# A macaron layer with routed experts on one core: weights sent by SyncE behind x, row numbers read and fetched by GpSimd, and a new order of the work

## The chip, the cores and the metric

The kernel runs on one core of a Trainium2 chip. The metric is device time in microseconds of one execution, the median of several. Five engines have work: TensorE (PE; its weight loads are PEld), VectorE (DVE), ScalarE (ACT), GpSimd (POOL) and SyncE (SP), which only issues transfers. Each engine runs its instructions in order, and a wait at the head of an engine holds all that is queued behind it.

## The reference

x has 8 sequences of 512 tokens of 256 numbers, 4,096 tokens in all. The layer is feed-forward, attention, feed-forward, each added to x:

```python
x = x + 0.5 * ffn(layernorm(x), gate_w, w1, w2, w3)
x = x + attn(layernorm(x), W_q, W_k, gain, bias, log_mix, log_scale)
x = x + 0.5 * ffn(layernorm(x), gate_w, w1, w2, w3)   # the same weights again
```

`ffn` scores 8 experts per token, keeps the best two, and for these two computes `w2 @ (silu(w1 @ t) * (w3 @ t))` with an inner width of 512, weighted and summed. `attn` compares each token with the earlier ones of its sequence (x·x), keeps the 8 most alike, takes a softmax over q·k of these, blends the mean of their vectors with x, and passes gain, bias and a gelu. Both need the whole precision of float32 in the choice of experts and of neighbours, so the kernel splits numbers into a high and a low float16 part and multiplies three times.

## The kernel before

**The two feed-forward layers** (L = 0 and 1) are computed only for chosen experts. Tokens are taken in "subtiles" of 512 (8 per layer, n = 0 to 7 for L = 0 and 16 to 23 for L = 1): layer norm (`stats`, `aggr` on DVE, the root `root` on POOL at L903, `shift` on DVE, `normal` and `nhi` on ACT, `low` on DVE), the gate (`flip`, `flop`, `score`), the choice (`rcopy`, `rtop`, `rsel`, `rank`, `rpos`). Then `scatter` writes each token's row (high and low parts and the token's number) to a list of its expert in DRAM, `hs`, by indirect transfers of POOL (L921): two of 128 rows for each `scatter`, 32 `scatter` and so 64 transfers a layer. The second choice (k = 1) first waits until the first choice's transfers of the same rows have landed, since it rewrites the token numbers in place (L918).

**Tables and tiles.** `table` computes on DVE which expert and which 128 rows each tile takes. Layer 0 has two tables: the first after the first quarter of the tokens is known, for tiles 0 to 8; the second needs all 64 transfers and nine padding writes (`pads`, SP), and serves tiles 9 to 70. `line` (SP) copies a table's row numbers into one partition, `rows` (SP, L1008) loads them into registers of SP, up to four tiles at a time. There are 71 tiles a layer, 142 in all, numbered through. For each tile n:

- `load` on SP: wait for the scatters and for the buffer, then turn 128 rows of `hs` into `HT` (ring of 3) by a transposing transfer (L991), and fetch the 128 row numbers into `IDX` (ring of 8) by a plain one of 4 bytes a row (L995);
- `up` on PE (L1161): two halves of 6 products of 512 columns; `tanh` (silu, ACT L1289), `gate` (DVE L1654), `high` (ACT L1298), `glow` (DVE L1660);
- `gt` on SP (L1031): a transposing transfer into `GH` (ring of 3); `down` on PE (L1173): 12 products of 256 columns; `evict` (ACT L1305, ring of 3);
- `put` on POOL (L939): an indirect transfer that writes the result rows to `yt`, where the tokens' order is restored.

**The weights** (12.6 MB, six transfers of 2 MB) come in on POOL's queue, issued behind the third `root` (L907). PE sums their squares (`sum`, L1097), DVE makes scales (`scale`), ACT and DVE split each of 24 pieces (`wh`, `wl`; L1239, L1457). The first `up` needs 16 pieces split, the first `gt` and `down` all 24 (`s_wl` 24).

**The middle**: `fetch` (SP L1046) and `join` (DVE L1669) bring a layer's results back into x; for each of 8 sequences the attention steps follow (`ht`, `qk`, `sim`, `sco`, `top`, `veil`, `mask`, `exp`, `phi`, `plo`, `pt`, `msg`, `blend`, and on POOL `affine`, L948 and L951), interleaved with tiles of layer 0 and the routing of layer 1. At the end the joins of layer 1 and the outputs (`out`, SP L1069).

**The order** of all this is one string, `ORDER`, a letter for each step. A small planner (`make_plan`) replays it, checks that each step's predecessors are there, and hands out the PSUM banks and buffers; each engine then runs its own steps in that order.

Of the kernel before, what the change touches and what calls it, by code (L numbers as in the profile page):

```python
# [9 lines left out]
F32 = mybir.dt.float32  # L10
# [17 lines left out]
RING = 8  # L28
# [65 lines left out]
class Want:  # L94
# [9 lines left out]
LAG = 3  # L104
PS = 1
# [147 lines left out]
def make_plan():  # L253
# [224 lines left out]

    def loads():
        for n, (L, j) in enumerate(seq):  # L480
            k = table_for(L, j)
            use["tab", n] = k
            known = (L, KNOWN[L][k])
            r = router_at(*known)
            after = (("table", (L, k)),) + tuple(("scatter", last_scatter(L, f)) for f in range(r[1] + 1))
            after += (("pads", (L, 8)),) if KNOWN[L][k] == NT else ()
            after += (("rows", (head[n],)),)
            yield tile("load", (n,), after + ((("up", (n - 3, 1)),) if n >= 3 else ()) +
                       ((("put", (n - RING,)),) if n >= RING else ()))

# [13 lines left out]
    def tanhs():  # L504
        for n in range(N):
            yield tile("tanh", (n,), (("up", (n, 0)),) + ((("glow", (n - 2,)),) if n >= 2 else ()),
                       gives=(("x", n, 0),))
# [17 lines left out]
    def evicts():  # L525
        for n in range(N):
            yield tile("evict", (n,), (("down", (n,)),) + ((("put", (n - 3,)),) if n >= 3 else ()),
                       gives=(("y", n),))
# [5 lines left out]
    P.run([prepare(), final(), first_routers(), tables(0), tables(1), sums(), scales(), split(), split2(),  # L534
           scalars(), rows(), loads(), whiches(), ups(), downs(), tanhs(), gates(), highs(), glows(), turned(),
# [4 lines left out]
def macaron_kernel(nc, x_d, wk_d, wqk_d, gw_d, gain_d, bias_d, lg_d, out_d, hs_d, yt_d):  # L540
    P, seq = make_plan()
    use, nth = P.use, P.nth
    with ExitStack() as ctx:
# [108 lines left out]
        HT = [sb(f"ht{i}", [128, 512], F16) for i in range(3)]  # L652
        TH = [sb(f"th{i}", [128, 512], F32) for i in range(2)]
# [14 lines left out]
        d_in = [sem(f"d_in{i}") for i in range(3)]  # L668
        d_y = [sem(f"d_y{i}") for i in range(3)]
# [6 lines left out]
        d_gt = [sem(f"d_gt{i}") for i in range(3)]  # L676
# [137 lines left out]
        def stored(n):  # L814

            return [16 * ((n - i) // 3 + 1) for i in range(3)]
# [45 lines left out]
        def _(eng):  # L862
            e = Eng(eng)
            const, marks, zeros = Tick(s_const), Tick(s_mk1), Tick(s_zero)
# [33 lines left out]
            for kind, key in P.order:  # L898
                if kind == "root":
# [24 lines left out]
                elif kind == "zero":  # L924
# [5 lines left out]
                    zeros.on(eng.tensor_copy(PHS[slot][:, PADC:PADC + 18].bitcast(I32), padid[:]))  # L930
                elif kind == "put":
# [4 lines left out]
                    if j > FULL:  # L936
                        e.wait_ge(d_y[(n - 1) % 3], 16 * ((n - 1) // 3 + 1))
# [23 lines left out]
        def _(eng):  # L961
# [9 lines left out]
            for kind, key in P.order:  # L971
# [8 lines left out]
                elif kind == "load":  # L980
# [8 lines left out]
                    if n >= 3:  # L989
                        e.wait_ge(s_x3, n - 2)  # L990
# [793 lines left out]
```

## Time and profile before

| | us |
|---|---|
| median of 3 runs | 896.85 (896.12 to 900.83) |
| the profiled execution | 894.73 |
| its span | 893.0 |
| PE busy | 716.3 (80%) |
| DVE, ACT, POOL busy | 559.7, 512.6, 379.8 |

The span is the time from the first to the last instruction in the trace; the profiled execution's own time is 1.7 us more. "Busy" of POOL does not count its waits, register loads and the issue gaps. A wait is named after the event that ended it.

### The profile page before, as it was taken

What the parts mean: (1) busy time and instruction counts of PE and PEld (TensorE: products, weight loads), DVE (VectorE), ACT (ScalarE), POOL (GpSimd) and SP (SyncE); (2) the same over time, 40 slices, a digit from 0 to 9 for tenths busy, and PEclk for the clock granted to TensorE, in tenths of its full rate; (3) what the DMA queues carried; (4) which work ended last, traced back from release to release, by engine and by line L of the source; (5) the groups of instructions that cost most, each with busy time, mean ns of one, the idle gap of its engine ahead of it and who ended that gap; (6) DMA issues with size and microseconds to landing.
All of it is one profiled execution on the core that took longest, in us unless ns stands there. A gap on an engine that the chain in (4) does not pass through costs nothing. (4 is left out here: it accounts for less than half of the span.)

```text
span 893.0 us, 17410 instructions
## 1 busy us (share of the span) xinstructions
PE 716.3 (80%) x4672; PEld 432.9 (48%) x4672; DVE 559.7 (63%) x1596; ACT 512.6 (57%) x954; POOL 379.8 (43%) x433
## 2 busy tenths in 40 slices
PE   1652425799989998889998798889998889997971
PEld 1551213446645555554555455555554445654641
DVE  6728881233367786786879787888684514335753
ACT  4727831263357896866889688865874323332320
POOL 4447874213322325465365634564364522221211
PEclk9975588899999999999999999999999989999986
DMA  6953237466796878797987877797878677678995
GB/s 239 429 196 93 93 102 169 108 110 140 132 212 116 127 157 135 144 194 158 178 170 181 166 163 145 138 185 150 153 137 166 150 169 142 128 134 234 218 279 178
DMA packets 328213, 147.76 MB, mean 165 GB/s; under 512 B 309501, under 2 KB 312445, under 8 KB 327357
## 3 DMA queue, kind: packets, MB, share of 16 engines
q1 hardware_dynamic: 314301, 97.61, 57.2%
q0 software_dynamic: 13824, 49.04, 16.8%
q8 instruction: 47, 0.77, 0.4%
q14 instruction: 41, 0.34, 0.1%
HBM read 33.96 MB, written 43.14 MB: 86 GB/s over the span
## 5 line engine op out<-in xcount | busy, mean ns | idle before, releaser
L1161 PE MATMUL B<-t_W,t_ht 128*128 x1704 | 406.1, 388 | 49.5 <-DMA t_ht<-hs 38.6
L939 POOL DMA_INDIRECT yt<-t_W,t_idx x142 | 148.8, 1048 | 388.6 <-ACT t_W L1305 338.4
L1161 PEld LDWEIGHTS B<-t_W,t_ht 128*128 128x128 f16 x1704 | 167.4, 99 | 233.7 <-issue 75.8
L1654 DVE SCALAR_TENSOR_TENSOR t_th<-B,t_K,t_th 128x512 f32<-128x512 f32 x142 | 105.9, 748 | 134.5 <-PE B L1161 93.3
L1173 PE MATMUL B<-t_W,t_gh 128*128 x1140 | 142.8, 276 | 24.7 <-DMA t_gh<-t_gp 18.4
L1289 ACT ACTIVATE t_th<-B,t_K 128x512 f32<-128x512 f32 x142 | 96.8, 683 | 106.7 <-PE B L1161 89.1
L1173 PEld LDWEIGHTS B<-t_W,t_gh 128*128 128x128 f16 x1140 | 109.3, 99 | 61.0 <-issue 37.0
L921 POOL DMA_INDIRECT hs<-t_s,t_POS x112 | 117.1, 1045 | 47.7 <-issue 25.5
L1305 ACT ACTIVATE t_W<-B 128x256 f32<-128x256 f32 x142 | 53.1, 374 | 98.1 <-PE B L1173 87.4
L1660 DVE TENSOR_TENSOR t_gp<-t_th,t_gp 128x512 f16<-128x512 f32 x95 | 66.9, 707 | 32.6 <-ACT t_gp L1298 29.0
L1298 ACT ACTIVATE t_gp<-t_th 128x512 f16<-128x512 f32 x95 | 58.8, 624 | 42.1 <-DVE t_th L1654 28.1
L1173 PE MATMUL B<-t_W 128*128 x564 | 71.0, 276 | 5.5 <-ACT t_W L1305 2.9
L1173 PEld LDWEIGHTS B<-t_W 128*128 128x128 f16 x564 | 54.6, 99 | 22.2 <-issue 9.9
L1258 ACT ACTIVATE t_hp<-t_X,t_ve 128x256 f32<-128x256 f32 x96 | 49.5, 590 | 24.5 <-DVE t_ve L1503 24.0
L1660 DVE TENSOR_TENSOR t_W<-t_th,t_W 128x512 f16<-128x512 f32 x47 | 32.7, 695 | 26.7 <-ACT t_W L1298 21.2
L1289 ACT ACT_TABLE_LOAD x31 | 39.8, 1283 | 6.5 <-DVE t_gp L1660 3.6
L1298 ACT ACTIVATE t_W<-t_th 128x512 f16<-128x512 f32 x47 | 29.3, 624 | 21.5 <-DVE t_th L1654 19.4
L1669 DVE SCALAR_TENSOR_TENSOR t_X<-t_hp,t_CW,t_X 128x256 f32<-128x256 f32 x64 | 31.9, 508 | 14.4 <-DMA t_hp<-yt 13.3
L903 POOL TENSOR_TENSOR t_ve<-t_ve,t_mhalf 128x4 f32<-128x4 f32 x24 | 26.9, 1122 | 31.9 <-DVE t_ve L1497 31.1
L1669 DVE SCALAR_TENSOR_TENSOR t_X<-t_s,t_CW,t_X 128x256 f32<-128x256 f32 x64 | 30.4, 488 | 12.7 <-DMA t_s<-yt 11.6
L1514 DVE TENSOR_TENSOR t_s<-t_hp,t_s 128x256 f16<-128x256 f32 x88 | 36.1, 461 | 0.0
L1225 PE MATMUL B<-t_s,t_ph 128*128 128x256 f16 x240 | 31.3, 273 | 4.5 <-DMA t_ph<-t_p 3.8
(205 smaller groups left out, 855.3 us busy)
## 6 DMA issues: line engine op xcount, KB each, us to landing
t_W<-wk POOLq DMA_DIRECT2D x6, 2048.0 KB, 13.3
t_hp<-yt SPq DMA_DIRECT2D x16, 512.0 KB, 4.4
t_s<-yt SPq DMA_DIRECT2D x15, 512.0 KB
t_X<-x SPq DMA_DIRECT2D x8, 512.0 KB, 7.3
out<-t_X SPq DMA_DIRECT2D x7, 512.0 KB, 5.8
hs<-t_ph SPq DMA_DIRECT2D x18, 136.0 KB
t_ht<-hs SPq DMA_TRANSPOSE x142
t_idx<-hs SPq DMA_DIRECT2D x142, 0.5 KB
```

The lines of the kernel that those rows point to most:

```text
L921: eng.indirect_dma_start(hs_d[L], bass.IndirectOffsetOnAxis(ap=POS[:, k, t + j:t + j + 1], axis=0), SROW[slot][:, 2 * h + j, :], None).the ...
L939: eng.indirect_dma_start(yt_d[L], bass.IndirectOffsetOnAxis(ap=IDX[:, n % RING:n % RING + 1], axis=0), YO[n % 3], None).then_inc(d_y[n % 3 ...
L1161: t = eng.matmul(B[b][:], HT[n % 3][:, (2 * hl + db) * 128:(2 * hl + db) * 128 + 128], W16[:, bass.ds(expert[n] * 4096 + (db * 2048 + wl * ...
L1173: t = eng.matmul(B[b][:, 0:256], GH[n % 3][:, gl, fb * 128:fb * 128 + 128], W16[:, bass.ds(expert[n] * 2048 + (W2OFF + wl * 1024 + fb * 25 ...
L1258: eng.activation(hp[:, j, :], X[:, t0 + j, :], ACT.Identity, bias=ve[:, 2, j:j + 1], scale=ve[:, 1, j:j + 1]).then_inc(s_hp, 1)
L1289: eng.activation(TH[n % 2][:], B[b][:], ACT.Silu, scale=K[:, 0:1]).then_inc(free[b], 1)
L1298: eng.activation(GP[n % 3][:, 0, :], TH[n % 2][:], ACT.Copy).then_inc(s_gh, 1)
L1305: eng.activation(YO[n % 3], B[b][:, 0:256], ACT.Copy).then_inc(free[b], 1)
L1514: eng.tensor_tensor(s16[:, j, 256:512], hp[:, j, :], s16[:, j, 0:256], ALU.subtract).then_inc(s_lo, 1)
L1654: eng.scalar_tensor_tensor(out=th[:], in0=B[b1][:], scalar=K[:, 7:8], in1=th[:], op0=ALU.mult, op1=ALU.mult).then_inc(free[b1], 1)
L1660: eng.tensor_tensor(gp[:, 1, :], th[:], gp[:, 0, :], ALU.subtract).then_inc(s_gl, 1)
L1669: xs.on(eng.scalar_tensor_tensor(out=X[:, tile, :], in0=yg[:, k, :], scalar=CW[:, k, tile:tile + 1], in1=X[:, tile, :], op0=ALU.mult, op1= ...
```

## The change

1. **Weights.** POOL no longer issues them behind `root` 2; SP does, behind x, the small weights, lg and bias, at the start.
2. **Row numbers.** `load` on SP keeps only the transposing transfer. The plain transfer into `IDX` becomes a step `ids` on POOL, with the same waits for the scatters, the pads and the buffer. POOL gets the row numbers in registers of its own by a step `places`, which loads them as SP's `rows` does. `rows` stays. `IDX` becomes a ring of 16 instead of 8. `put` now needs `ids` instead of `load`.
3. **Order.** `ORDER` is a new string. The other ring sizes get names (HTR, YR, THR, LAG) and keep their values.

```diff
-RING = 8
+RING = 16
...
+HTR = 3
+YR = 3
+THR = 2
...
+    def place():
+        for i, g in enumerate(groups):
+            L, j = seq[g[0]]
+            yield tile("places", (g[0],), (("line", (L, table_for(L, j))),))
+
+    def idents():
+        for n, (L, j) in enumerate(seq):
+            yield tile("ids", (n,), ready(n) + (("places", (head[n],)),) +
                        ((("put", (n - RING,)),) if n >= RING else ()))
...
-            yield tile("put", (n,), (("evict", (n,)), ("load", (n,))) + ((("put", (n - 1,)),) if seq[n][1] > FULL else ()))
+            yield tile("put", (n,), (("evict", (n,)), ("ids", (n,))) + ((("put", (n - 1,)),) if seq[n][1] > FULL else ()))
...
@@ gpsimd @@
-                    if n == 2:
-                        e.wait_ge(d_x[5], 16)
-                        for i in range(6):
-                            eng.dma_start(W[:, 4 * i + 2:4 * i + 6, :],
-                                          wk_d[:, 4 * i:4 * i + 4, :]).then_inc(d_w[i], 16)
...
+                elif kind == "places":
+                    n, = key
+                    L, j = seq[n]
+                    e.wait_ge(d_line[L][table_for(L, j)], 16)
+                    _, regs = nc.values_load_multi_w_load_instructions(
+                        LINE[L][0:1, j:j + len(group[n])], engines=[mybir.EngineType.Pool], min_val=0, max_val=SPARE,
+                        skip_runtime_bounds_check_because="the table's rows are cut off at the spare one")
+                    place.update(zip(group[n], regs))
+                elif kind == "ids":
+                    n, = key
+                    L, j = seq[n]
+                    k = table_for(L, j)
+                    for s, v in scattered(*router_at(L, KNOWN[L][k])):
+                        e.wait_ge(s, v)
+                    if KNOWN[L][k] == NT:
+                        e.wait_ge(d_pad, 144 * (L + 1))
+                    if n >= RING:
+                        e.wait_ge(d_y[(n - RING) % YR], 16 * ((n - RING) // YR + 1))
+                    eng.dma_start(IDX[:, n % RING:n % RING + 1].bitcast(F16), hs_d[L][bass.ds(place[n], 128), 512:514]
+                                  ).then_inc(d_id[n % RING], 16)
...
@@ sync @@
             eng.dma_start(bias[:], bias_d).then_inc(d_bias, 16)
+            for i in range(6):
+                eng.dma_start(W[:, 4 * i + 2:4 * i + 6, :], wk_d[:, 4 * i:4 * i + 4, :]).then_inc(d_w[i], 16)
...
-                    if n >= 3:
-                        e.wait_ge(s_x3, n - 2)
-                    eng.dma_start(HT[n % 3][:].rearrange("p (a b) -> p a b", a=4), hs_d[L][bass.ds(row, 128), 0:512],
-                                  transpose=True).then_inc(d_in[n % 3], 16)
-                    if n >= RING:
-                        e.wait_ge(d_y[(n - RING) % 3], 16 * ((n - RING) // 3 + 1))
-                    eng.dma_start(IDX[:, n % RING:n % RING + 1].bitcast(F16), hs_d[L][bass.ds(row, 128), 512:514]
-                                  ).then_inc(d_id[n % RING], 16)
+                    if n >= HTR:
+                        e.wait_ge(s_x3, n - HTR + 1)
+                    eng.dma_start(HT[n % HTR][:].rearrange("p (a b) -> p a b", a=4), hs_d[L][bass.ds(row, 128), 0:512],
+                                  transpose=True).then_inc(d_in[n % HTR], 16)
```

The two strings, read engine by engine, hold the same steps but for 38 `places` and 142 `ids`. Where they differ most, around the end of layer 0's scatters (steps numbered in order on their engine; `scatter` 31 is the last of layer 0):

```
POOL before: ... scatter25 scatter26 scatter27 put0 scatter28 scatter29 put1 put2 scatter30 put3 put4 scatter31 put5 put6 ...
POOL after:  root5 places0 scatter6 ... scatter13 root7 ids0 places1 ids1 scatter14 places2 ids2 scatter15 ...
             ... scatter27 scatter28 put0 scatter29 places3 put1 scatter30 ids3 ids4 ids5 scatter31 put2 put3 ids6 ids7
             places4 ids8 ids9 ids10 ids11 put4 places5 ids12 ids13 ids14 places6 put5 ...
SP before:   load2 rows2 load3 gt0 load4 load5 pads0 pads1 line1 gt1 ... gt5 pads8 gt6 gt7 load9
SP after:    load2 rows2 load3 load4 load5 line1 pads0 gt0 gt1 ... gt5 pads8 rows3 gt6 load9
PE before:   up3 up4 down0 down1 up5 down2 up6a down3 down4 up6b up7 down5 up8 down6 down7 up9
PE after:    up3 up4a down0 up4b up5a down1 up5b up6a down2 up6b up7a down3 up7b down4 up8 down5 down6 up9
```

Later the two orders run side by side: at `table` 2 (the first of layer 1) both have issued 71 `up` and 66 `put`, at the last `scatter` 111 and 110 `up`. The `ids` stand in runs of one to five.

## Rows read from the trace of the kernel before

**Rows 1.** The page: busy time of the engines
```profile
PE 716.3 (80%) x4672; PEld 432.9 (48%) x4672; DVE 559.7 (63%) x1596; ACT 512.6 (57%) x954; POOL 379.8 (43%) x433
```
**Rows 2.** Busy time by stretch: stretch, length, five engines, PE clock, DMA share, GB/s
```profile
40.00:50.00 10.00, 5.75 (x56) 5.26 (x57) 3.01 (x13) 1.75 (x6) 3.03 (x4) 0.68 1.03 405
50.00:60.00 10.00, 5.71 (x101) 5.53 (x98) 0.00 (x0) 1.02 (x1) 4.90 (x7) 0.98 0.45 167
...
450.00:500.00 50.00, 45.07 (x302) 27.16 (x299) 43.87 (x142) 42.95 (x82) 27.83 (x31) 1.00 0.77 168
```
**Rows 3.** Timeline of POOL, 42 to 54 us: start, length, work, idle before
```profile
42.98 0.96 POOL L921 DMA_INDIRECT hs<-t_s,t_POS  x1 [0.31 <-issue]
53.90 0.19 POOL L918 COPY t_s<-t_ids 128x2 int32<-128x2 int32 x1 [9.96 <-DMA hs<-t_s,t_POS]
```
**Rows 4.** Timeline, 60 to 61 us: DVE behind POOL's root
```profile
60.40 0.17 DVE L1503 SCALAR_TENSOR_TENSOR t_ve<-t_mv,t_ve 128x4 f32<-128x4 f32 x1 [10.43 <-POOL t_ve L903]
```
**Rows 5.** Timeline of SP, PE and ACT, 130 to 168 us: tiles 0, 1, 4, 6
```profile
130.16 1.24 SPq L1031 DMA_TRANSPOSE t_gh<-t_gp  x1
...
131.54 1.59 SPq L991 DMA_TRANSPOSE t_ht<-hs  x1
...
136.14 4.22 PE L1161 MATMUL B<-t_W,t_ht 128*128 x12 [15.54 <-DMA t_ht<-hs]
...
140.34 1.28 SPq L1031 DMA_TRANSPOSE t_gh<-t_gp  x1
...
145.24 0.38 ACT L1305 ACTIVATE t_W<-B 128x256 f32<-128x256 f32 x1 [2.05 <-issue]
...
167.40 2.61 SPq L1031 DMA_TRANSPOSE t_gh<-t_gp  x2
```
**Rows 6.** Timeline of POOL, 131 to 171 us: puts between the last scatters
```profile
131.22 1.34 POOL L921 DMA_INDIRECT hs<-t_s,t_POS  x1 [0.30 <-issue]
...
142.87 0.96 POOL L939 DMA_INDIRECT yt<-t_W,t_idx  x1 [10.30 <-ACT t_W L1305]
...
146.59 0.32 POOL L918 COPY t_s<-t_ids 128x2 int32<-128x2 int32 x1
...
149.72 0.96 POOL L939 DMA_INDIRECT yt<-t_W,t_idx  x1 [0.30 <-issue]
...
160.96 0.96 POOL L939 DMA_INDIRECT yt<-t_W,t_idx  x1 [5.47 <-ACT t_W L1305]
...
169.23 1.11 POOL L921 DMA_INDIRECT hs<-t_s,t_POS  x1 [0.30 <-issue]
```
**Rows 7.** Timeline of SP and PE, 173 to 178 us: tile 9
```profile
173.41 2.02 SPq L991 DMA_TRANSPOSE t_ht<-hs  x1
...
177.39 11.85 PE L1161 MATMUL B<-t_W,t_ht 128*128 x48 [2.92 <-DMA t_ht<-hs]
```
**Rows 8.** Prices by line: shortest, median, longest ns; then first and last start
```profile
L1008 SPq TENSOR_LOAD <-t_line x38: 300/952/1869, 44.9 to 849.1; - x38
...
L907 POOL DMA_DIRECT2D t_W<-wk x6: 537/537/797, 18.1 to 21.1; - x6
...
L939 POOL DMA_INDIRECT yt<-t_W,t_idx x142: 954/960/1766, 142.9 to 882.6; - x142
...
L995 SPq DMA_DIRECT2D t_idx<-hs x142: 333/437/1453, 70.5 to 857.0; - x142
```
**Rows 9.** Waits of PE, 165 to 850 us: total, times, longest
```profile
PE B L1161 <- DMA t_ht<-hs: 18.7, 11, 5.3
```
**Rows 10.** Waits of POOL, 450 to 500 us, the same columns
```profile
POOL yt L939 <- ACT t_W L1305: 7.8, 4, 2.6
POOL yt L939 <- issue: 5.0, 4, 3.3
POOL t_ve L903 <- DVE t_ve L1497: 4.5, 2, 2.5
...
POOL hs L921 <- DVE t_POS L1588: 2.4, 1, 2.4
```

More of the change, by code:

```diff
@@ L152 @@
+    "F*FS.**;E>WUUPF;JJ;NSP.NSUPQ>EF;;.NSPUUUJQg1gQ**EF**JUUUUEFQEFJJUUUUJJ~**gJgUUUUg1ggg")
 class Plan:
@@ L477, in rows, with ready @@
             yield tile("rows", (g[0],), (("line", (L, table_for(L, j))),) + ((("load", (groups[i - 1][0],)),) if i else ()))
+    def ready(n):
+        L, j = seq[n]
+        k = table_for(L, j)
+        return ((("table", (L, k)),) + tuple(("scatter", last_scatter(L, f)) for f in range(router_at(L, KNOWN[L][k])[1] + 1)) +
+                ((("pads", (L, 8)),) if KNOWN[L][k] == NT else ()))
     def loads():
         for n, (L, j) in enumerate(seq):
[L481 to L488, printed above, removed]
+            use["tab", n] = table_for(L, j)
+            yield tile("load", (n,), ready(n) + (("rows", (head[n],)),) + ((("up", (n - HTR, 1)),) if n >= HTR else ()) )
+    def place():
[5 more added lines that the diff above has]
+            yield tile("ids", (n,), ready(n) + (("places", (head[n],)),) +
                        ((("put", (n - RING,)),) if n >= RING else ()))
@@ L505, in tanhs @@
         for n in range(N):
-            yield tile("tanh", (n,), (("up", (n, 0)),) + ((("glow", (n - 2,)),) if n >= 2 else ()),
+            yield tile("tanh", (n,), (("up", (n, 0)),) + ((("glow", (n - THR,)),) if n >= THR else ()),
                        gives=(("x", n, 0),))
@@ L526, in evicts @@
         for n in range(N):
-            yield tile("evict", (n,), (("down", (n,)),) + ((("put", (n - 3,)),) if n >= 3 else ()),
+            yield tile("evict", (n,), (("down", (n,)),) + ((("put", (n - YR,)),) if n >= YR else ()),
                        gives=(("y", n),))
@@ L651, in macaron_kernel @@
         AT = [sb(f"at{i}", [128, 16], F32) for i in range(4)]
-        HT = [sb(f"ht{i}", [128, 512], F16) for i in range(3)]
-        TH = [sb(f"th{i}", [128, 512], F32) for i in range(2)]
+        HT = [sb(f"ht{i}", [128, 512], F16) for i in range(HTR)]
+        TH = [sb(f"th{i}", [128, 512], F32) for i in range(THR)]
         wqs = [P16[:, 256 + 128 * i:384 + 128 * i].rearrange("p (a b) -> p a b", a=2) for i in range(2)]
@@ L667, in macaron_kernel @@
         d_gw, d_qk, d_lg, d_gain, d_bias = (sem(n) for n in ("d_gw", "d_qk", "d_lg", "d_gain", "d_bias"))
-        d_in = [sem(f"d_in{i}") for i in range(3)]
-        d_y = [sem(f"d_y{i}") for i in range(3)]
+        d_in = [sem(f"d_in{i}") for i in range(HTR)]
+        d_y = [sem(f"d_y{i}") for i in range(YR)]
         d_sc = [[sem(f"d_sc{i}{h}") for h in range(2)] for i in range(5)]
@@ L675, in macaron_kernel @@
         d_ph = [sem(f"d_ph{i}") for i in range(2)]
-        d_gt = [sem(f"d_gt{i}") for i in range(3)]
+        d_gt = [sem(f"d_gt{i}") for i in range(LAG)]
         d_g = [[sem(f"d_g{i}{h}") for h in range(2)] for i in range(6)]
@@ L814, in stored @@
         def stored(n):
-            return [16 * ((n - i) // 3 + 1) for i in range(3)]
+            return [16 * ((n - i) // YR + 1) for i in range(YR)]
         def joined(L, tile):
@@ L1286, in _ @@
                     e.wait_ge(s_kk, N_K1)
-                    if n >= 2:
-                        e.wait_ge(s_gl, n - 1)
-                    eng.activation(TH[n % 2][:], B[b][:], ACT.Silu, scale=K[:, 0:1]).then_inc(free[b], 1)
+                    if n >= THR:
+                        e.wait_ge(s_gl, n - THR + 1)
+                    eng.activation(TH[n % THR][:], B[b][:], ACT.Silu, scale=K[:, 0:1]).then_inc(free[b], 1)
                 elif kind == "high":
@@ L1301, in _ @@
                     e.wait_ge(s_y, n + 1)
-                    if n >= 3:
-                        e.wait_ge(d_y[n % 3], 16 * (n // 3))
+                    if n >= YR:
+                        e.wait_ge(d_y[n % YR], 16 * (n // YR))
                     b, turn, _ = use["y", n]
-                    eng.activation(YO[n % 3], B[b][:, 0:256], ACT.Copy).then_inc(free[b], 1)
+                    eng.activation(YO[n % YR], B[b][:, 0:256], ACT.Copy).then_inc(free[b], 1)
                 elif kind == "qkout":
@@ L1648, in _ @@
                     n, = key
[L1649 removed]
+                    th = TH[n % THR]
                     b0, turn0, _ = use["x", n, 0]
```

91 lines of the change are left out of this document (46 added, 45 removed), and 2 rows, old and new, of the table KINDS.

## The prediction

> **What bounds the kernel now.** I read the page first: PE is busy for 716.3 of 893.0 us [rows 1], so 177 us are PE's idle time, and the question is where it lies. The table of stretches answers it. In the middle PE is full but for a tenth: 45.07 of 50 us from 450 to 500 [rows 2]. A gain there could come only from PE's last waits, and those for `HT`, the buffer that SP fills, are 18.7 us in all from 165 to 850 [rows 9]. Most of the idle time lies ahead of tile 9, whose `up` starts a dense run at 177.39 [rows 7]. So the timeline of the start is what has to be read, backwards from there.
>
> Tile 9's `load` is issued at 173.41, because it needs layer 0's last scatter, which POOL issues from 169.23 to 170.34 [rows 6, 7]; the landing takes 173.41 - 170.34 = 3.1 us, and the turned tile is there 4.0 us after its issue. So **POOL's queue is the chain ahead of tile 9**, and POOL loses time on it in three places.
>
> First, from 43.94 on it stands 9.96 us [rows 3]: `scatter` 4 rewrites numbers that `scatter` 0 is still sending, and the latter's transfers, issued behind 12.6 MB of weights (from 18.1 us on, L907 of [rows 8]), have not landed. The DMA engines are then full (405 GB/s, share 1.03 from 40 to 50 us) and fall to 0.45 in the next ten [rows 2]. VectorE stands behind the same wait: it has no work from 50 to 60 us [rows 2] and resumes at 60.40 when POOL has made the root queued behind these scatters, having idled 10.43 us for that alone [rows 4].
>
> Second, 28 of 32 scatter steps are out at 131.22 + 1.34 = 132.56, and then POOL stands 10.30 us for `put` 0 [rows 6]. That put's chain is `gt` 0 at 130.16 (it needs all weights split), but PE does `up` 3 and 4 ahead of `down` 0 and sits 15.54 us, until 136.14, for tile 4's load, which SP holds behind `gt` 0 and issues about then [rows 5].
>
> Third, puts 2 to 4 stand between the last scatters; `put` 3 waits 5.47 us [rows 6], `put` 4 some more.
>
> **Part 1, the weights on SP.** SP's list is empty until the first line, so issuing costs nothing: its cover is that idle time, and uncovered it would be six issues of about the 0.54 us that they cost on POOL [rows 8]. The transfers start when x is in instead of at 18.1 us. At the observed 405 GB/s [rows 2] 12.6 MB take 31 us, so the weights are in some 5 to 8 us earlier, near 45 us (an estimate from these rows). What counts more is that POOL's scatters are no longer behind them in one queue. I take the stand away whole: `scatter` 4 starts at 42.98 + 0.96 + 0.28 = 44.2 instead of 53.90, **-9.7 us** on POOL's chain; the least is -5, if the landing still has to wait for the full engines to empty, the most -10. The Trainium skill (DMA: Bandwidth & Descriptors, "Queues, rings and completion order") says that each DMA engine goes round robin between queues, packet by packet; by that rule the scatters interleave with the weights and the whole 9.96 us go, where a reading by full engines alone leaves about half. VectorE gets about the same 10 us, as its wait ended with POOL's. Late next there is DVE's splitting of the weights: all split at about 130.1 - 10.4 = 119.7.
>
> **Part 2, the numbers on POOL.** A `places` is the register load that SP does in 0.95 us at the median, 0.30 to 1.87 at the ends [rows 8]; 38 of them. For an `ids` there is no row on POOL. Bounds: the plain weight transfer at 0.54 us and the indirect one at 0.96 plus its gap of 0.30, at worst 1.77 + 0.30 [rows 6, 8]. I take 0.8, nearer the plain form, which it has. SP loses 142 issues of 0.44 us [rows 8]; where SP was the last thing waited for, that is worth a part of 18.7 us [rows 9], of which I take 1 to 2. On the chain ahead of tile 9 lie `places` 0 to 3 (3.8 us) and `ids` 0 to 5 (4.8 us): **+8.6 us**, from 4.5 to 20 by the bounds. The wait that `places` 0 adds, for the line that SP sends behind the weights, ends near 45 to 47 us; POOL comes there after two scatters and a root, at about 44.2 + 5.3 + 1.1 = 50.6, so it is free, though behind it would be scatter 6. Over the rest, 136 `ids` and 34 `places` are 136 x 0.8 + 34 x 0.95 = 141 us of POOL in 720 us. Their cover is POOL's waits: from 450 to 500 us, a full stretch, 7.8 + 5.0 + 4.5 + 2.4 = 19.7 us [rows 10], against 9.8 us added in 50. Behind an `ids` stand puts, roots and the affine steps; puts have a ring of three. I take +1 to +2, which cancels SP's relief; the ends for both together are -4 and +12.
>
> **Part 3, the order.** Its worth at the start can be worked out. A scatter step is 149.72 - 146.59 = 3.1 us [rows 6] with its copy; I use 3.0. New POOL chain: 132.56 - 9.7 + 3.0 (`scatter` 28 now ahead of `put` 0) + 2.9 (`places` 0 to 2) + 2.4 (`ids` 0 to 2) = 131.1 for `put` 0. Is that put ready? All weights are split at 119.7; `down` 0 follows one half `up`, and from `gt` 1's issue at 140.34 to the end of its eviction at 145.62 are 5.3 us [rows 5], so it is ready at about 125: no wait. Then `put` 0 1.3, `scatter` 29 3.0, `places` 3 1.0, `put` 1 1.3, `scatter` 30 3.0, `ids` 3 to 5 2.4, `scatter` 31 3.0 give 146.1, against 170.34. With 3.1 and 4.0 us as above, POOL lets tile 9 start at 153.2. SP has a bound of its own: `gt` 6 stands ahead of load 9. From `gt` 1 to `gt` 6 before it is 167.40 - 140.34 = 27.1 us, 5.4 each [rows 5]; from 119.7 six of them end at 152.1, and load and landing make 157. That pace held waits for POOL that now go, so I take the middle near the later end, 156. That is 177.4 - 156 = **-21.4 us**. PE then still owes one `down` more than before, +1.5. From tile 9 on the two orders run alike, and since PE is full there its whole work moves forward. The new string could be better or worse by some PE gaps; nothing in the rows prices this, and I keep 5 us to either side.
>
> **The sum.** 894.73 - 21.4 + 1.5 + 0 = 874.8 for a profiled execution, which lies 2.1 us under the median of the runs; so 877 for the median.
>
> **The rivals.** (a) The stand at 44 us stays by half, since the DMA engines are full until 45 us either way [rows 2]; for it speaks the share of 1.03, against it that the weights themselves now end 5 to 8 us sooner. Part 1 then gives 5 us less: 882.
>
> (b) The start's gain is given back: what follows is not held by PE alone but also by the attention's chain and by transfers, and the roots and affine steps behind `ids` come later. For it: DVE and ACT are busy 43.87 and 42.95 of 50 us [rows 2]. Against: PE has more than either and these all shift with the start. At about half given back, 887.
>
> (c) Slower: POOL becomes the bound in the middle. Its spare time from 450 to 500 us is 19.7 us [rows 10]; ten `ids` and 2.7 `places` fill that when an `ids` costs 1.6 us and a `places` 1.87 (16 + 5 = 21). Past that point puts come late, `evict` waits for its ring of three and PE for the bank. At 2.1 us an `ids` (the worst row with its gap) it is 21 + 5 = 26, 6 us too many in each 50; over the 250 us that are so full, 30 us: 877 + 30 = 907. The Trainium skill (DMA: Bandwidth & Descriptors, "SWDGE vs HWDGE vs iDMA") says that GpSimd builds descriptors in SBUF and can be locked out by VectorE, which SyncE's transfers cannot; by that rule `ids` is dearer exactly where DVE is busiest. The trace bears it out in part: the indirect transfers go from 0.96 to 1.77 us [rows 8], but the median stays at the low end.
>
> (d) The change does not bite: the first part is not on the path, because DVE's 24 splits and routing, not POOL, set when tile 9 can start, and the new order only shuffles. DVE was full before and after its stand. Then at most 3 us are gained: 894.
>
> **How the numbers follow.** The forecast has 0.66, its own range 868 to 884. Rival (a) 0.10, (b) 0.11, (c) 0.06, (d) 0.07. A measurement of this kernel tells 0.5% from no change, that is 4.5 us: faster means under 892.4, slower over 901.3. Faster: forecast, (a), nearly all of (b): 0.86. Same: (d) and the rest of (b): 0.08. Slower: (c): 0.06. The range for 8 in 10: below, the stand gone, `ids` at 0.6 us, the later end's SP bound not binding and 5 us of better order, 866; above, (a) and most of (b), 889.
>
> **What would show it.** After: POOL without a wait of more than 3 us between scatters 0 and 28; DVE not empty from 50 to 60 us; all weights split near 120; the last scatter of layer 0 near 146; tile 9's `up` near 156, and the same time saved at its end. An `ids` at 0.5 to 1.0 us on POOL. PE busy some 716 us again. Wrong, if the last scatter ends after 160, if an `ids` takes over 1.5 us, or if tile 9 is early by 20 us and the end is not.

## The result, and the profile after

The changed kernel takes 839.73 us (median of 4 runs, 836.57 to 843.08) against 898.84 (896.12 to 902.61) beside it: ratio 0.934, interval 0.929 to 0.939. The forecast was 877, its range 866 to 889. The sign and the start were right; the gain is 59 us where 20 were forecast. Times are medians of every execution made; ratios leave out the few that ran in a slower state of the chip.

The page of the changed kernel, the busy times (before: [rows 1]) and the line of GpSimd's new transfers:
```profile
PE 700.0 (84%) x4672; PEld 429.8 (51%) x4672; DVE 557.4 (67%) x1596; ACT 506.6 (61%) x950; POOL 457.3 (55%) x569
...
L957 POOL DMA_DIRECT2D t_idx<-hs x142 | 80.4, 571 | 10.2 <-DMA yt<-t_W,t_idx 5.1
```
POOL carries 77 us more and an `ids` costs 0.57 us. Nothing else took on work, and the same 4672 matmuls are done.

Timeline of POOL at the start, changed kernel. The first two rows answer to [rows 3], the rest to [rows 6]:
```profile
44.25 0.96 POOL L929 DMA_INDIRECT hs<-t_s,t_POS  x1 [0.30 <-issue]
46.53 0.19 POOL L926 COPY t_s<-t_ids 128x2 int32<-128x2 int32 x1 [1.32 <-DMA hs<-t_s,t_POS]
...
129.90 0.97 POOL L967 DMA_INDIRECT yt<-t_W,t_idx  x1 [1.50 <-ACT t_W L1331]
...
141.46 1.00 POOL L929 DMA_INDIRECT hs<-t_s,t_POS  x1 [0.30 <-issue]
```
Scatter 4 no longer waits for landings (its rewriting starts at 42.50); of the stand of 9.96 us a wait of 1.32 is left, one scatter on. `put` 0's wait of 10.30 is 1.50, and layer 0's last scatter has left at 142.46 instead of 170.34. DVE, idle throughout from 50 to 60 us in [rows 2], now works there; after it stand SP and PE at tile 9 (before: [rows 7]):
```profile
50.00:60.00 10.00, 4.05 (x44) 3.97 (x45) 8.50 (x38) 6.85 (x12) 6.67 (x9) 0.50 0.34 75
```
```profile
122.20 3.01 SPq L1057 DMA_TRANSPOSE t_gh<-t_gp  x2
...
148.75 2.52 SPq L1021 DMA_TRANSPOSE t_ht<-hs  x2
```
```profile
152.99 5.34 PE L1187 MATMUL B<-t_W,t_ht 128*128 x24
...
811.51 1.72 PE L1199 MATMUL B<-t_W,t_gh 128*128 x12
```
Tile 9's `up` starts at 152.99 instead of 177.39: 24.4 us, 21.4 forecast. PE's last matmul ends at 813.23. In the kernel before it is this one, at 874.60:
```profile
873.13 1.47 PE L1173 MATMUL B<-t_W,t_gh 128*128 x12
```
So from tile 9 to the last matmul it took 697.2 us and takes 660.2: **37 us of the gain lie where the forecast had none.** After the last matmul stand 18.4 us before and 21.4 after, so the spans differ by 24.4 + 37.0 - 3.0 = 58.4 us (893.0 and 834.6).

That middle as one stretch, before and after (columns as in [rows 2]):
```profile
177.39:875.00 697.61, 634.26 (x3998) 377.26 (x3998) 452.06 (x1224) 428.84 (x820) 279.81 (x295) 0.98 0.80 162
```
```profile
152.99:816.00 663.01, 625.56 (x4012) 377.85 (x4009) 453.52 (x1245) 422.60 (x818) 353.54 (x425) 0.99 0.86 171
```
PE's busy time falls by 8.7 us (the granted clock is 0.99 where it was 0.98) and its idle time, counted to the last matmul, from 63 to 35 us. What filled the gaps? The forecast had asked PE's waits. SP's own waits tell more. First the kernel before, 200 to 800 us, then the changed one (total, times, longest):
```profile
SPq L1031 <- DVE t_gp L1660: 11.9, 15, 1.6
SPq L1031 <- DVE t_W L1660: 6.9, 8, 1.5
SPq L62 <- DVE t_p L1715: 6.3, 7, 2.3
SPq L978 <- DVE t_s L1514: 3.8, 4, 1.4
```
```profile
SPq L1057 <- DVE t_gp L1686: 25.2, 25, 3.1
SPq L62 <- DVE t_p L1741: 18.6, 11, 4.6
SPq L62 <- PE B L1199: 11.5, 9, 2.5
SPq L1021 <- PE B L1187: 9.2, 8, 3.1
```
All rows of this view together, smaller ones included, give 36.6 us of waits in 600 before and 90.5 after. **Before, SP waited for only 6% of the middle: it was at least as full as PE**, with instructions that the page does not count as busy. (A rough count agrees: some 120 loads and 120 `gt` of these 600 us and the 80 transposes of the attention at about 1.25 us, 120 row-number transfers at 0.44, the register loads, and gaps of 0.1 to 0.2 us between them come to about 560.) The timeline of SP before, in a full stretch:
```profile
458.23 1.58 SPq L991 DMA_TRANSPOSE t_ht<-hs  x1
460.00 0.44 SPq L995 DMA_DIRECT2D t_idx<-hs  x1
460.56 1.19 SPq L991 DMA_TRANSPOSE t_ht<-hs  x1
461.94 0.44 SPq L995 DMA_DIRECT2D t_idx<-hs  x1
462.50 1.22 SPq L991 DMA_TRANSPOSE t_ht<-hs  x1
463.90 0.44 SPq L995 DMA_DIRECT2D t_idx<-hs  x1
464.45 1.24 SPq L1031 DMA_TRANSPOSE t_gh<-t_gp  x1
465.79 1.20 SPq L1063 DMA_TRANSPOSE t_ph<-t_p  x1
467.08 1.26 SPq L1031 DMA_TRANSPOSE t_W<-t_W  x1
```
One transfer is issued behind the other with a gap of 0.1 to 0.2 us; a row-number transfer takes a slot of 0.56 us (461.94 to 462.50). 142 of these are 80 us of SP's time. The Trainium skill (Perfetto Trace Analysis, "What "DMA-bound" means") names this case: the issuing engine's own track is solid DMA slices, which are the making of descriptors and not the moving of data. The trace agrees in the solid track: from 458.23 to 468.34 no gap is longer than 0.19 us. What an issue spends its time on, no run here shows.

### The profile page after: what moved, and what is told of

Its sections match the earlier page's. It is cut to its first block and busy times, and to the rows that moved or that the text cites. A ratio compares the mean times of both kernels' runs of the same rounds, so it can differ in the third digit from the quotient of the medians.

```text
span 834.6 us, 17466 instructions
## 1 busy us (share of the span) xinstructions
PE 700.0 (84%) x4672; PEld 429.8 (51%) x4672; DVE 557.4 (67%) x1596; ACT 506.6 (61%) x950; POOL 457.3 (55%) x569
## 5 line engine op out<-in xcount | busy, mean ns | idle before, releaser
L1187 PE MATMUL B<-t_W,t_ht 128*128 x1704 | 399.0, 382 | 29.5 <-DMA t_ht<-hs 10.4
L1315 ACT ACTIVATE t_th<-B,t_K 128x512 f32<-128x512 f32 x142 | 96.6, 682 | 68.5 <-PE B L1187 48.4
L957 POOL DMA_DIRECT2D t_idx<-hs x142 | 80.4, 571 | 10.2 <-DMA yt<-t_W,t_idx 5.1
L1686 DVE TENSOR_TENSOR t_W<-t_th,t_W 128x512 f16<-128x512 f32 x47 | 32.5, 692 | 16.6 <-ACT t_W L1324 12.3
L976 POOL TENSOR_TENSOR t_hp<-t_hp,t_W 128x256 f32<-128x256 f32 x32 | 27.2, 850 | 23.8 <-DVE t_hp L1758 23.4
L1540 DVE TENSOR_TENSOR t_s<-t_hp,t_s 128x256 f16<-128x256 f32 x88 | 33.5, 430 | 1.3 <-ACT t_s L1294 1.3
```

Of the source, the lines that this page charges most:

```text
L957: eng.dma_start(IDX[:, n % RING:n % RING + 1].bitcast(F16), hs_d[L][bass.ds(place[n], 128), 512:514]).then_inc(d_id[n % RING], 16)
L1187: t = eng.matmul(B[b][:], HT[n % HTR][:, (2 * hl + db) * 128:(2 * hl + db) * 128 + 128], W16[:, bass.ds(expert[n] * 4096 + (db * 2048 + wl ...
L1315: eng.activation(TH[n % THR][:], B[b][:], ACT.Silu, scale=K[:, 0:1]).then_inc(free[b], 1)
L1540: eng.tensor_tensor(s16[:, j, 256:512], hp[:, j, :], s16[:, j, 0:256], ALU.subtract).then_inc(s_lo, 1)
L1686: eng.tensor_tensor(gp[:, 1, :], th[:], gp[:, 0, :], ALU.subtract).then_inc(s_gl, 1)
```

## The experiments

Each time was taken beside runs of the kernel before on the same chip. The latter's medians were 896.8, 894.9, 896.7 and 894.2 in the four groups below and 898.8 beside the changed kernel, so a difference between runs of two groups, all that are taken from 839.7 among them, is uncertain by some 2 to 5 us. Ratios are to the kernel before of the same group, with their 95% intervals.

**First group: which part.** Theory T: the gain behind tile 9 is the new order's. Theory R: it is the relief of SP.

Weights alone: the kernel before with
```
-                    if n == 2:
-                        e.wait_ge(d_x[5], 16)
-                        for i in range(6):
-                            eng.dma_start(W[:, 4 * i + 2:4 * i + 6, :],
-                                          wk_d[:, 4 * i:4 * i + 4, :]).then_inc(d_w[i], 16)
...
+            for i in range(6):
+                eng.dma_start(W[:, 4 * i + 2:4 * i + 6, :], wk_d[:, 4 * i:4 * i + 4, :]).then_inc(d_w[i], 16)
```


> The kernel before with part 1 alone: SyncE sends the weights, order and row numbers as they were. The stand of 9.96 us on POOL at 44 us should go. Both theories (the order made the rest of the gain; the relief of SyncE made it) say the same here: layer 0's last scatter some 10 us earlier than 170.3, and 886 to 890 us for a median of 898.8. If 5 us or less are gained, the weights' queue was not on the path of the old order.

Measured 892.2, ratio 0.996 (0.992 to 1.000): 4.6 us, less than expected and hardly clear of nothing. By the expectation's own words the weights' queue was then not on the path of the old order. The stand at scatter 4 is gone in this run too, and scatter 6 goes out 9.8 us earlier (50.98 for 60.81). But scatter 8 follows at 67.66, where it was at 68.78. Its rows on DVE and POOL, and under them POOL's in the kernel before and in the changed one:
```profile
57.06 0.29 DVE L1522 TENSOR_REDUCE t_rta<-B 128x64 f32<-128x128 f32 x1 [14.73 <-remote]
67.66 1.04 POOL L916 DMA_INDIRECT hs<-t_s,t_POS  x1 [10.60 <-DVE t_POS L1585]
```
```profile
68.78 1.04 POOL L921 DMA_INDIRECT hs<-t_s,t_POS  x1 [1.67 <-DVE t_POS L1588]
```
```profile
58.70 1.04 POOL L929 DMA_INDIRECT hs<-t_s,t_POS  x1 [1.87 <-DVE t_POS L1614]
```
**A second wait of the same length stood behind the first.** In the old order PE works through sums of the weights' squares, many of them one at a time between 40 and 53 us, before it computes the gate scores at 53.06 that VectorE's choice needs; VectorE resumes at 57.06, and POOL waits 10.60 us for the positions. So 1.1 us is left of the 9.8. `put` 0 takes back nothing: its wait is 9.97 us for 10.30. The new order has scatter 8 out 10 us earlier, and at 60.17 in a run below with the row numbers still on SP. That the sums hold PE up is read from the order of its rows; no run moved them alone.

The old order in the changed code, so parts 1 and 2 without 3. The edit is in the string `ORDER` alone: the old one, with a `places` put behind each `rows` and an `ids` behind each `load`.

> The changed kernel's code with the old order: each places stands right behind its rows, each ids right behind its load. Parts 1 and 2 without part 3. Theory T (behind tile 9 the new order makes the gain): about 885 to 892, since ids cost POOL 0.57 us each and SyncE's relief is worth little. Theory R (behind tile 9 the gain is SyncE's relief of 142 transfers and the longer ring): the start's 10 us and most of the 34 us behind tile 9, so 855 to 862.

Measured 870.1, ratio 0.974 (0.965 to 0.982), between what the two theories expected. Taking the row numbers off SP is worth 22 us in the old order. This step also lengthens the ring of `IDX` from 8 to 16, which no run in the old order took apart. The trace of before bounds the ring's share: from 200 to 800 us SP waited there for an old put by
```profile
SPq L995 <- DMA yt<-t_W,t_idx: 1.8, 2, 1.1
```

The new order without part 2. This is the code before with the weights on SP, `RING = 16` and the new string without its `places` and `ids`, so that SP's `load` again ends with
```
                     if n >= RING:
                         e.wait_ge(d_y[(n - RING) % 3], 16 * ((n - RING) // 3 + 1))
                     eng.dma_start(IDX[:, n % RING:n % RING + 1].bitcast(F16), hs_d[L][bass.ds(row, 128), 512:514]
                                   ).then_inc(d_id[n % RING], 16)
```


> The new order and the weights on SyncE, but the row numbers fetched by SyncE within load, as before (with the ring of 16, which the order needs). T: within 5 us of the changed kernel's 839.7, so 838 to 846. R: the 34 us behind tile 9 are lost, so 865 to 875.

Measured 887.7, ratio 0.991 (0.987 to 0.996). **Theory T falls.** The time lies 13 us above theory R's range too: R priced the loss too low. Without part 2 the new order is worth 4.5 us (892.2 to 887.7, with intervals that overlap), with it 30 (870.1 to 839.7). Part 2 is worth 22 in the old order and 48 in the new, where both versions have the ring of 16.

The changed kernel with the weights back on GpSimd, the edit of the first experiment turned round:

> The changed kernel with part 1 undone: POOL sends the weights behind the third root. T and R: the stand of about 10 us at 44 us is back and all behind it is 8 to 11 us later, so 848 to 851. If under 3 us are lost, the weights' queue did not matter in the new order.

Measured 854.6, ratio 0.953 (0.944 to 0.961): part 1 is worth 15 us here, more than expected and three times its worth alone. The traces say where: scatter 8 starts 10.8 us later (69.52 for 58.70), layer 0's last scatter starts 12.3 us later (153.79 for 141.46) and tile 9 11.5 us later (164.45 for 152.99), so here no second wait takes the gain back.

**Second group: what it is about SP.** Three mechanisms could make the row numbers dear there: the time in SP's queue (Q), the 128 small packets each between transposes (D), or the wait for an old put that stood ahead of them (W).

The changed kernel, one transfer more behind each load, to a scratch tile nobody reads:
```
                                   transpose=True).then_inc(d_in[n % HTR], 16)
+                    if n >= 8:
+                        e.wait_ge(d_du[n % 8], 16 * (n // 8))
+                    eng.dma_start(DUM[0:128, n % 8:n % 8 + 1].bitcast(F16),
+                                  hs_d[L][bass.ds(row, 128), 512:514]).then_inc(d_du[n % 8], 16)
```


> The changed kernel, in which SyncE sends one plain transfer more behind each of the 142 loads, of the same form as the row numbers' (128 rows of 4 bytes), to a scratch tile that nobody reads; nothing waits for it. Theory Q (what the row numbers cost was time in SyncE's queue, some 0.44 us of issue each, 62 us in all, in a queue that is nearly full): the time goes back to about that of the new order with the row numbers on SyncE, 870 to 890 us. Theory D (it was the 18,176 small packets that stand between the transposes on the same queue): 870 to 890 too. Theory W (it was the wait for an old put that stood in SyncE's order ahead of the transfer): 838 to 846, as nothing waits here.

Measured 881.4, ratio 0.985 (0.979 to 0.991): +41.7 us.

The same with `DUM[0:1, ...]` and `bass.ds(row, 1)`:

> The same, but the extra transfer takes one row of 4 bytes, so that SyncE issues as many instructions, with 1 descriptor in place of 128. Theory Q: within 8 us of the run with 128 rows, if the issue of a small transfer holds SyncE as long; if its issue is shorter in the trace, in proportion to it. Theory D: 838 to 850. Theory W: 838 to 846.

Measured 872.8, ratio 0.977 (0.971 to 0.983): +33.1 us. The timelines of SP, first with 128 rows, then with one:
```profile
449.89 1.19 SPq L1023 DMA_TRANSPOSE t_ht<-hs  x1
451.27 0.44 SPq L1027 DMA_DIRECT2D t_dum<-hs  x1
451.82 0.39 SPq L1078 DMA_DIRECT2D t_hp<-yt  x1
```
```profile
460.02 1.19 SPq L1023 DMA_TRANSPOSE t_ht<-hs  x1
461.40 0.30 SPq L1027 DMA_DIRECT2D t_dum<-hs  x1
461.81 1.24 SPq L1063 DMA_TRANSPOSE t_W<-t_W  x1
```
The slot is 0.55 us with 128 rows and 0.41 with one. 142 slots are 78 and 58 us, of which 41.7 and 33.1 reach the end: 53 and 57%. So the cost follows SP's time, not the packets. The pages count 20,448 packets more on SP's queue with 128 rows and 284 more with one; this takes back 8.6 us, about as much as the shorter issue explains (20 us of slots). Theory D falls. The section of the Trainium skill cited above says that for a full issuing track large descriptors are what matters. No run here made them larger. One row in place of 128 of the same size took back a fifth of the 41.7 us, so four fifths go with the number of issues, whether each carries 128 rows or one.

The wait alone, behind the transfer in SyncE's `load`:
```
+                    if n >= RING:
+                        e.wait_ge(d_y[(n - RING) % YR], 16 * ((n - RING) // YR + 1))
```


> The changed kernel, in which SyncE waits behind each load for the put of 16 tiles before, as it did ahead of the row numbers, and sends nothing more. Theories Q and D: within 3 us of the changed kernel, 837 to 843. Theory W: 860 or more.

Measured 839.5, ratio 0.940 (0.933 to 0.946): nothing. Theory W falls for the new order, with the ring of 16 that was tested; for the old one there is the row above of 1.8 us.

Part 2 alone, in the old order with the weights on GpSimd:

> The kernel before with its old order and its weights on GpSimd, in which only the row numbers and their registers went to GpSimd (a ring of 16). With the weights on SyncE this was 870.1 us and the weights alone gained 4.6, so with parts that add up it is 872 to 877; with the start behind GpSimd's weights and more on GpSimd, 878 to 884.

Measured 879.2, ratio 0.983 (0.977 to 0.989): 15.7 us of gain, in the second of the two ranges: the parts do not simply add up. The weights on SP then bring 9 more (870.1), twice what they bring alone.

**Third group: more relief, and the order cut in two.** Groups of up to 8 tiles read by one register load:
```
-        if g and len(g) < (2 if n < 3 else 4) and seq[g[0]][0] == L and table_for(L, seq[g[0]][1]) == table_for(L, j):
+        if g and len(g) < (2 if n < 3 else 8) and seq[g[0]][0] == L and table_for(L, seq[g[0]][1]) == table_for(L, j):
```


> The changed kernel, in which SyncE and GpSimd each read the places of up to 8 tiles with one load into registers in place of up to 4 (20 loads each in place of 38), the order kept but for the steps dropped. Theory Q says that time taken off SyncE's queue comes back in part: 18 loads fewer of 1.3 us at the median (23 us), of which a tenth to a third, since SyncE now waits 98 us in the middle and TensorE only some 37: 832 to 838 us. A theory in which SyncE has stopped to matter once the row numbers are gone: 838 to 842.

Measured 852.3, ratio 0.953 (0.947 to 0.959): 12.6 us slower, against both forecasts. The loads, before this edit and with it (ns: shortest, median, longest):
```profile
L1034 SPq TENSOR_LOAD <-t_line x38: 328/1274/2117, 48.0 to 782.8; - x38
```
```profile
L1034 SPq TENSOR_LOAD <-t_line x20: 676/1923/2960, 48.4 to 775.4; - x20
```
On SP 48 us became 38 (count times median), a small saving, and SP's waits stay at 89.6 us; on POOL the median went from 0.97 to 2.39 us and the longest from 2.4 to 4.4. That the longer stops are what costs is an argument, not shown. Theory Q's forecast for this edit was wrong in any case: the runs bear it out for what is put on SP, and not for what is taken off once SP waits 90 of 600 us.

The 33 fetches moved to ScalarE (the `fetch` branch moved, in its words unchanged), on top of that:

> The run before, and ScalarE sends the 33 transfers that fetch the tokens' results (0.35 us of issue each on SyncE, 12 us, and SyncE's waits for the puts ahead of them). Theory Q: 0 to 6 us less than the run before. Against it: ScalarE waits in its own order for those puts, and its tanh and gelu work stands behind them: then 5 to 20 us more.

Measured 882.3, ratio 0.986 (0.980 to 0.993): 30 us more. The case against it expected 5 to 20; that waits for puts in front of ScalarE's work are what costs was not followed in the trace. SP's waits rise to 121.5 us, so a still emptier SP does not help by itself. Of these versions none beats the changed kernel.

The new order up to tile 9's `up`, the old one behind it, and the reverse:

> The changed kernel with the new order up to the first half of tile 9's up-projection and the old order, the row numbers in it as in x5, from there on. If the new order gains by its start alone, which stood 17 us earlier at tile 9 than with the old order (152.99 against 169.83), 850 to 856. If what it gains lies behind tile 9, 864 to 872.

> The other half: the old order up to tile 9's first half, the new one from there on. By the start 864 to 870; by what stands behind tile 9 852 to 858. If the two parts add up, the two runs lie as far above 839.7 together as the old order did, 30 us.

Measured 861.8 (0.961, 0.956 to 0.967) and 868.2 (0.970, 0.964 to 0.975). Neither half does it: they lie 22 and 28 us above the whole, 50 together, where the two orders differ by 30. From tile 9 on, though, each half behaves like its own order: the new one behind the old start takes 667.0 us to the last matmul (660.2 in the whole), the old one behind the new start 687.7 (679.1).

**Fourth group: controls.** As many extra transfers of 128 rows as above, but issued by ScalarE, behind each tile's `tanh`; they read x instead of `hs`, and 8 bytes a row instead of 4:
```
                     eng.activation(TH[n % THR][:], B[b][:], ACT.Silu, scale=K[:, 0:1]).then_inc(free[b], 1)
+                    if n >= 8:
+                        e.wait_ge(d_du[n % 8], 16 * (n // 8))
+                    eng.dma_start(DUM[:, 2 * (n % 8):2 * (n % 8) + 2], x_d[:, n % 8, 0:2]
+                                  ).then_inc(d_du[n % 8], 16)
```


> The changed kernel and 142 plain transfers more of 128 rows of 8 bytes, as in the run with the extra transfer of 128 rows, but issued by ScalarE behind each tile's tanh, from x to a scratch tile. Theory Q (SyncE's queue): no more than ScalarE's own issue can cost, 840 to 852, far below the 881.4 of the same transfers on SyncE. If any extra work or the packets themselves upset the new order, 865 or more.

Measured 838.3, ratio 0.938 (0.931 to 0.946): nothing, with this row in the trace:
```profile
L1322 ACTq DMA_DIRECT2D t_dum<-x x142: 334/335/398, 101.6 to 807.3; - x142
```
The page counts 20,448 packets more, as many as with the extra transfers on SP. **142 transfers of 128 small rows cost 42 us on SP and none on ScalarE.** It is the time in SP's queue, and not the DMA engines, the number of packets or just any extra work.

The extra single-row transfer (`DUM[0:1, ...]`, as above) in the old order, which took 870.1 without it:

> The changed code in the old order (870.1 us) and one transfer of a single row behind each load on SyncE. Theory Q with a price of its own per order (the row numbers cost 22 us in the old one, 48 in the new): two thirds of 22, 880 to 887. If each issue costs alike in both orders, 900 to 905, 33 us more as in the new order.

Measured 880.3, ratio 0.986 (0.979 to 0.993): +10.2 us, where the new order paid 33.1 for the same. The lower of the two expectations, at its edge.

The new order up to tile 71, the old one behind it:

> The changed kernel in the new order up to tile 71's up-projection (of 142), the old one from there on. If the gain of the new order is spread over the tiles, half of what lies between 861.8 (new up to tile 9) and 839.7 (new throughout) is back, 848 to 853. If a change from one order to the other costs something at the seam itself, 856 or more.

Measured 853.9 (847.8 to 860.6), ratio 0.954 (0.946 to 0.963), between the two expectations and between 861.8 (seam at tile 9) and 839.7 (no seam). It fits a gain spread over the tiles; the interval is too wide to exclude a few us at the seam.

**All of it in one table**, from the profiled executions: where tile 9's `up` starts, how long it is from there to the last matmul, and the waits from 200 to 800 us, summed over all rows of the view.

| kernel | tile 9 | to last matmul | SP waits | PE waits |
|---|---|---|---|---|
| before | 177.4 | 697.2 | 36.6 | 48.5 |
| old order, weights on SP, row numbers too | 172.5 | 703.4 | 46.3 | 53.1 |
| old order, row numbers off SP | 169.8 | 679.1 | 97.1 | 44.3 |
| the same, one-row transfer on SP | 162.9 | 696.7 | 51.9 | 48.4 |
| new order, row numbers on SP | 161.6 | 706.4 | 45.2 | 58.3 |
| changed kernel | 153.0 | 660.2 | 90.5 | 30.2 |
| the same, weights on GpSimd | 164.5 | 667.5 | 81.2 | 30.1 |
| new order to tile 9, then old | 157.4 | 687.7 | 101.1 | 43.9 |
| old order to tile 9, then new | 178.1 | 667.0 | 77.1 | 32.4 |
| extra on SP, 128 rows | 154.1 | 707.7 | 48.8 | 56.2 |
| extra on SP, one row | 156.5 | 694.4 | 48.8 | 48.4 |
| extra on ScalarE | 156.6 | 660.9 | 89.2 | 30.2 |

Wherever a small transfer per tile stands on SP, SP's waits are 37 to 52 us and the middle takes 694 to 708, whichever order it is. With SP relieved its waits are 77 to 101, and then the order behind tile 9 decides: 679 to 688 with the old one, 660 to 668 with the new. Each row is one execution, and the column of tile 9 scatters: the old order with the row numbers off SP, the same steps up to tile 9, has 169.8 in one row and 178.1 in another, and 162.9 with a transfer more; the new one has 153.0 to 157.4. The middle scatters less: the changed kernel with only the wait more, which took no more time, has 665.8 in its trace for 660.2. Differences smaller than these should not be read.

## Why the prediction was wrong, and where it was right

**Part 1.** Half right. The stand went (1.32 us left), DVE works from 50 to 60 us, and all weights are split by 122.1 (119.7 forecast). The six issues on SP take 0.7 us each under the cover named:
```profile
7.92 4.30 SPq L999 DMA_DIRECT2D t_W<-wk  x6
```
But the "-9.7 us on POOL's chain" was taken as part 1's own. By itself it leaves 1.1 us at scatter 8 and 1.9 when POOL comes to `put` 0, since POOL's next wait, for positions that hang on PE's scores, takes its place; it is worth 4.6 us. The forecast looked one wait ahead. The 10 us came because the new order moves that wait too, and then part 1 is worth 15: the number was right for the two together, which for part 1 was luck.

**Part 3 at the start.** Right: `put` 0 at 129.9 (131.1), the last scatter out at 142.5 (146.1), tile 9 at 153.0 (156), each a little early; of the 3.6 us at the scatter 1.4 are six `ids` at 0.57 us for 0.8, the rest is spread. SP's bound also showed: load 9 is issued 6.3 us after the last scatter, not 3.1, as a `pads`, `rows` 3 and a `gt` stand between.

**Part 2 is the step that failed**, and in it the sentence "where SP was the last thing waited for, that is worth a part of 18.7 us [rows 9], of which I take 1 to 2", with the lower end of -4 for both together. In its place the runs show 16 us alone, 22 beside part 1 and 48 in the new order. The premise failed with it, that in the middle "a gain there could come only from PE's last waits". The error was to price the relief of a queue by PE's waits for one of the tiles that it fills. SP also carries `gh`, `ph` and `hta`, for which PE waited too; that a late SP reaches PE through DVE and ACT as well, to which PE's waits are then put down, is argued and was not followed in a trace. Had SP's own waits been listed, as POOL's were [rows 10], 36.6 us in 600 would have shown an engine that waits for only 6% of the time. POOL's side was priced rightly: `ids` 0.57 us, `places` 0.97, and rival (c) had little ground: from 200 to 800 us ACT waited 8.7 us for puts, and ACT and DVE 2.3 and 3.8 for POOL's results (9.2 and 1.2 before).

**"From tile 9 on the two orders run alike"** failed with it. With SP relieved, the new order's middle is 19 us shorter than the old one's (660.2 against 679.1) and its start 12 to 25 us earlier in these traces; with SP full, its middle is no shorter at all (706.4 against 703.4). The term of 5 us to either side for the order fits an SP that stays full. Why the new order gains only when SP is relieved was not followed in the traces. The sum took the parts one by one; they do not add up, and the gain of the third exists only behind the second.

**PE "full".** "Since PE is full there" rested on 45.07 busy of 50 us [rows 2]. The tenth that is left is 63 us over the middle, more than the whole forecast gain. It bounds a gain from above and says nothing of how much of it can be had; once SP's queue was being emptied, the range should have left room for a good part of it.

**"PE busy some 716 us again"**: 700.0. Of the 16 us, 8.7 lie in the middle, where the granted clock is 0.99 for 0.98 (both near the higher of its two levels, 2.4 GHz); the rest lies outside it.

**The rivals.** (a), (b) and (d) expected less gain than the forecast and (c) a loss; none had the case that occurred, a hidden engine that is freed. Rival (d)'s mechanism, that routing and not POOL sets the pace, is near to what the old order shows with part 1 alone (892.2 us; 894 named).

Open: which steps of the new order make its middle shorter, and why the two halves together lose 50 us and not 30 (the middle behind a seam is 7 to 9 us longer than that of the whole order; the rest lies at the start, in the scatter of single traces). Positions of loads, puts and attention steps shift together, and no run took them apart. Also whether the row numbers could go to ScalarE instead, as the control suggests; it was not tried.

## What to carry to other kernels

List the waits of every engine that issues transfers, SyncE too, before pricing work moved off or onto it: its issuing does not count as busy, so a queue that waits 6% of the time looks idle on the page. Price a moved instruction by its slot in that queue times the share of such slots that reaches the end, and expect that share to hang on the order (here half to three fifths in the new order, 18 to 28% in the old), and bound the gain by all of the bound engine's idle time, not by its waits for one tile. Where a change both frees an engine and reorders the work, cost the order against the freed engine: the two parts do not add. And when a wait is taken away, look for the next one on the same engine before its length is booked as a gain: here one of 10.60 us stood behind one of 9.96.

## What was not expected of the hardware

- An issue on SP takes 0.29 us for one row of 4 bytes and 0.44 for 128 of them, two thirds for a 128th of the rows; a transposing one takes 1.2 us. On ScalarE 128 rows of 8 bytes took 0.335 us, on GpSimd 128 rows of 4 bytes 0.57.
- A register load of up to 8 values took 1.92 us on SP where up to 4 took 1.27, and 2.39 against 0.97 on GpSimd, at the median.
- GpSimd's 142 plain transfers kept to 0.57 us (0.53 to 0.65) although DVE is busy for two thirds of the span; the lock-out weighed in the prediction did not show in them.
